# An edge kernel's attribute encoding: two matmuls over 111 rows and 512 columns for four over 30 rows and 256

## The chip, the cores and the metric

The kernel runs on one core of one Trainium2 chip. The metric is the device time of one execution in microseconds; lower is better. Engines: PE (TensorE, matmuls; PEld are its weight loads), DVE (VectorE), ACT (ScalarE), POOL (GpSimd, which here issues the indirect gathers), SP (SyncE, which issues most other DMAs).

## The reference

A graph attention layer over 6250 nodes and 200000 edges sorted by destination, then a mixture of experts that the change does not touch. What matters is the encoding of an edge's three attributes and its use:

```python
h = (x @ W.T).reshape(n, H, D)          # H = 8 heads of 32
alpha = einsum(h_src, a_src) + einsum(h_dst, a_dst)
enc = relu(edge_attr @ edge_W.T + edge_b).reshape(-1, H, D)
alpha = alpha + jnp.sum(enc * h_dst, axis=-1)
alpha = where(alpha >= 0, alpha, 0.2 * alpha)
attn = softmax of alpha over the edges of one dst
out = segment_sum(h_src * attn[..., None], dst)
```

## The kernel before

Edges are laid out in rows of W = 4 ways: a row belongs to one node, a block has P = 128 rows, that is SLOTS = 512 edge slots, and there are 440 blocks. A step of the edge loop handles Q = 4 blocks, so there are 110 steps, written out one after another; GROUPS = 4 groups of 128 blocks hold the tables.

**Attributes.** To keep f32 precision in bf16, an attribute is split in three bf16 parts (`part_attrs`: cast, subtract, cast, subtract, cast), which gives KA = 9 rows a slot. `store_attrs` writes them with one DMA to `block_attr` in DRAM, as 9 rows of 512 slots for each block; the slots of a row's four ways lie side by side. `load_attr` of the edge loop brings a step's 9 x 2048 values in three times (36 KB each), under each other into `attrT`; with three rows of ones for the bias that makes KE = 30 rows. `keep["expander"]` holds the weights [30, 256] in three bf16 parts, copied there by six small DMAs of POOL.

**PE.** `front(q, b)` encodes block b of step q: for each way k it takes the 128 slots of that way (every fourth column of `attrT`) as stationary operand and `expander` as moving operand, four matmuls of 256 columns (L1036) into the PSUM tiles p_enc, two to a tile, a semaphore after each pair. Then it picks the block's node rows with a one-hot matmul, p_pick (L1043). `add_up` (L1065) sums the weighted source rows, four f32 matmuls a block. PE's order in a step is fixed: turn_rows, front(1), add_up of the step before (2), turn_back, front(2), add_up (3), front(3), add_up(0), front of the step after, add_up(1).

**DVE.** `front` multiplies p_enc by the node rows `near` (L1210, two a block) and reduces (L1214); `scores`, `scan`, `fall` and four `weigh` (L1260) follow in a fixed order. After each of the first 19 steps of every 32, `expand` works on the next group's table: 16 parts of moving words and attributes, then `part_attrs` (L204, L206, L208). ACT copies p_pick to `near` (L1132), makes the one-hot matrices and copies sums. POOL gathers 16 times a step (L1003) and waits for `near` and `weighted`. SP loads two steps ahead and stores the sums; at step 22 of each group it stores the next group's table (L120 to L128) once DVE has made it.

**Prologue.** It ends on group 0: `part_attrs` in ids_in's memory (L204), SP's L128, then the table of bases out (L375) and back (L377), a wait for all table stores, and the edge loop begins with DVE's memset of attrT to ones (L1388), for which SP's first loads wait. Earlier, POOL issues the copies to `expander` (L445, L446) between two gathers (L434, L439); the second needs `run_i` from DVE (L693).

Of the kernel before, what the change touches and what calls it, by code (L numbers as in the profile page):

```python
# [59 lines left out]
KE = 3 * (KA + 1)  # L60
# [64 lines left out]
def store_attrs(nc, scr, b0, n, parts, stored):  # L125

    block = bass.ds(b0, n) if not isinstance(b0, int) else slice(b0, b0 + n)
    nc.sync.dma_start(scr["block_attr"].rearrange("c (b s) -> b c s", s=SLOTS)[block, :, :], parts[0:n, :, :]).then_inc(stored, 16)  # L128
# [69 lines left out]
def part_attrs(nc, x, i, attrs, parts):  # L198


    of = parts[:, EF * i:EF * (i + 1), :]
    x.wait()
    if i < 2:
        x.link(nc.vector.tensor_copy(of, attrs))  # L204
        x.wait()
        x.link(nc.vector.tensor_tensor(attrs, attrs, of, ALU.subtract))  # L206
    else:
        x.link(nc.vector.tensor_copy(of, attrs))  # L208


def prologue(nc, a, scr, keep):

    with Scope(nc) as m:
# [47 lines left out]
        enc_left = m.sb("enc_left", [KA + 1, D])  # L261
# [30 lines left out]
            dummy_made dummy_stored bias_loaded merge_consts""".split()  # L292
# [29 lines left out]
        def _(sp):  # L322
# [56 lines left out]
            sp.wait_ge(s["table_stored"], 64)  # L379
# [3 lines left out]
        def _(pool):  # L383
# [10 lines left out]
            ins.then_inc(s["consts_made"], 1)  # L394
            nc.gpsimd.memset(ones[:, :], 1.0).then_inc(s["consts_made"], 1)
# [46 lines left out]

            pool.wait_ge(s["enc_split"], 4)
            for j in range(3):
                pool.dma_start(keep["expander"][KA * j:KA * (j + 1), :], enc_p[0:KA, j, :]).then_inc(s["enc_moved"], 16)  # L445
                pool.dma_start(keep["expander"][3 * KA + j:3 * KA + j + 1, :], enc_p[KA:KA + 1, j, :]).then_inc(s["enc_moved"], 16)  # L446
# [13 lines left out]
            pool.wait_ge(s["enc_moved"], 96)  # L460
# [227 lines left out]


# [109 lines left out]
def edge_loop(nc, a, scr, keep):  # L799

    with Scope(nc) as m:
        rec = m.sb("rec_in", [P, RING, Q, W + 1])
        rec_i = rec[:, :, :, :].bitcast(I32)
        attrT = m.sb("attrT", [KE, RING, Q, SLOTS], BF16)
# [77 lines left out]
        def _(sp):  # L882
# [10 lines left out]
            def load_attr(q):  # L893
                if q.since(RING):
                    sp.wait_ge(s["enc"], PAIRS * Q * (q.prev().s))
                cols = scr["block_attr"].rearrange("c (n e) -> n c e", e=Q * SLOTS)
                v = block_of(cols, q.s)
                for j in range(3):
                    sp.dma_start(attrT[KA * j:KA * (j + 1), q.par, :, :].rearrange("c q e -> c (q e)"), v).then_inc(s_attr[q.par], 16)
# [74 lines left out]
            for i in range(GROUPS - 1):  # L974
                for u in range(turn):
                    if u == LOADED_AT:
                        sp.wait_ge(s["table_stored"], 64 * (i + 1))
                    body(straight(RING + i * turn + u))
                    if u == STORED_AT:
                        store_group(i, P)  # L980
# [42 lines left out]
        def _(pe):  # L1023
            def front(q, b):
# [5 lines left out]
                for half in range(PAIRS):  # L1030
                    if PAIRS * b + half >= len(p_enc) or q.since(1):
                        pe.wait_ge(s["prod"], PAIRS * n + half + 1 - len(p_enc))
                    for j in range(2):
                        k = 2 * half + j
                        slots = attrT[:, q.par, b, :].rearrange("c (r k) -> c k r", k=W)[:, k, :]
                        last = nc.tensor.matmul(p_enc[(PAIRS * b + half) % len(p_enc)][:, j, :], slots, keep["expander"][:, :], start=True, stop=True)  # L1036
                    last.then_inc(s["enc"], 1)
# [163 lines left out]
        def _(dve):  # L1201
# [129 lines left out]
            def expand(i, k):  # L1331
# [12 lines left out]
                elif k == 2 * WAY_BITS:  # L1344
                    if i:
                        dve.wait_ge(s["table_stored"], 64 * i)
# [613 lines left out]
def build(nc, a, out):  # L1960
    def dram(name, shape, dt=F32):
# [4 lines left out]
               block_flags=dram("block_flags", (GROUPS * P, H, P)), block_places=dram("block_places", (GROUPS * P, P)), block_attr=dram("block_attr", (KA, GROUPS * P * SLOTS), BF16),  # L1966
# [11 lines left out]
def edge_part(nc, a, scr, whole):  # L1978
    with Scope(nc) as m:
        keep = dict(  # L1980
            whole, node_at=m.sb("node_at", [P, P]), expander=m.sb("expander", [KE, D], BF16),
# [45 lines left out]
```

## Time and profile before

| | |
|---|---|
| median of 3 runs | 3568.86 us (3564.5 to 3572.67) |
| the profiled execution | 3549.46 us |
| its span, first to last instruction | 3547.7 us |
| PE busy (matmuls) | 2421.1 us, 68% |
| PEld busy | 1634.9 us, 46% |
| DVE busy | 2273.3 us, 64% |
| ACT busy | 986.2 us, 28% |
| POOL busy | 1904.2 us, 54% |
| mean granted clock of PE | 0.763 of 2.4 GHz |
| edge loop | about 181 to 2990 us |

Busy time is from one profiled execution. Matmuls are pipelined and their ends are modelled, so the busy time of PE counts overlapping latency. What ended an idle stretch is inferred; "issue" is a wait that nothing in the profile explains.

### The profile page before, as it was taken

To read this page: it belongs to the slowest core of one execution; us is meant where nothing else is said; L and a number is where in the kernel's file an instruction comes from. 1 tells how busy PE (TensorE), PEld (TensorE's weight loads), DVE (VectorE), ACT (ScalarE), POOL (GpSimd) and SP (SyncE) were. 2 spreads that over 40 slices of the span, in tenths; PEclk is the share of its full clock that TensorE was granted. 3 is DMA by queue.
4 is the path that set the end of the run, shared out by engine and by line. 5 is a ranking of instruction groups with operands and counts; after the bars stand their busy time and mean duration, and the time that the engine had idled before them with its cause. 6 is when DMAs were issued, how large, how long until landed. Compare 5 with 4: busy or idle time off the path is not lost. (4 is left out here: it accounts for less than half of the span.)

```text
span 3547.7 us, 36332 instructions
## 1 busy us (share of the span) xinstructions
PE 2421.1 (68%) x8642; PEld 1634.9 (46%) x8642; DVE 2273.3 (64%) x3546; ACT 986.2 (28%) x2822; POOL 1904.2 (54%) x2041
## 2 busy tenths in 40 slices
PE   1647667776667667676677767777676554269998
PEld 1424444444444444444444444444444333168887
DVE  7957767776667677776667777776666554251223
ACT  3522222222222222222222222222222221043332
POOL 3656656666666566666666656666666442607000
PEclk9857777777778677877777777777777676559999
DMA  8355555556555555556555555556556883300000
GB/s 270 124 136 153 154 147 153 150 149 178 147 154 154 144 155 145 159 149 177 151 152 154 150 150 155 147 156 174 150 154 134 124 121 53 88 27 3 21 18 31
DMA packets 341609, 471.12 MB, mean 133 GB/s; under 512 B 115596, under 2 KB 262718, under 8 KB 341170
## 3 DMA queue, kind: packets, MB, share of 16 engines
q0 software_dynamic: 90000, 262.14, 30.0%
q1 hardware_dynamic: 250578, 206.73, 20.0%
q8 instruction: 60, 0.98, 0.1%
q14 instruction: 123, 1.01, 0.1%
q10 hardware_dynamic: 848, 0.26, 0.0%
HBM read 380.17 MB, written 88.72 MB: 132 GB/s over the span
## 5 line engine op out<-in xcount | busy, mean ns | idle before, releaser
L1003 POOL DMA_INDIRECT src_in<-t_node_rows,rec_in x1760 | 1681.5, 955 | 1112.4 <-issue 552.2
L1065 PE MATMUL p_sum<-weighted,hot 128*128 128x264 f32 x3520 | 1262.5, 520 | 610.5 <-issue 420.9
L1065 PEld LDWEIGHTS p_sum<-weighted,hot 128*128 128x128 f32 x3520 | 875.2, 259 | 975.6 <-issue 703.7
L1210 DVE SCALAR_TENSOR_TENSOR prod<-p_enc,near 128x512 f32<-128x512 f32 x880 | 563.1, 680 | 421.7 <-ACT near L1132 355.8
L1260 DVE TENSOR_TENSOR weighted<-src_in,p_turn 128x1024 f32<-128x1024 f32 x440 | 534.5, 1215 | 326.6 <-remote 129.8
L1214 DVE TENSOR_REDUCE dots<-prod 128x32 f32<-128x1024 f32 x440 | 536.9, 1220 | 15.2
L1043 PE MATMUL p_pick<-win,hotT 128*128 128x272 f32 x880 | 383.2, 523 | 192.5 <-ACT near L1132 88.3
L1112 ACT ACTIVATE hot<-apart 128x128 f32<-128x128 f32 x440 | 136.2, 309 | 1336.5 <-issue 543.8
L1132 ACT COPY near<-p_pick 128x272 f32<-128x272 f32 x440 | 169.4, 385 | 680.4 <-remote 391.3
L1036 PE MATMUL p_enc<-expander,attrT 30*128 30x256 bf16 x1760 | 314.7, 305 | 43.2 <-DMA attrT<-t_block_attr 42.9
L1043 PEld LDWEIGHTS p_pick<-win,hotT 128*128 128x128 f32 x880 | 154.2, 220 | 301.7 <-issue 200.9
L1036 PEld LDWEIGHTS p_enc<-expander,attrT 30*128 30x128 bf16 x1760 | 174.5, 121 | 190.8 <-issue 121.0
L1699 PE MATMUL p_up<-x2T,w 128*128 (+2 forms) x800 | 175.5, 378 | 9.3 <-DMA b<-in_L_ffn_b 9.3
L1108 ACT ACTIVATE apart<-node_at,rec_in 128x128 f32<-128x128 f32 x440 | 175.7, 399 | 0.0
L1709 PE MATMUL p_y<-w,act_h 128*128 128x256 f32 x784 | 173.1, 379 | 0.0
L1153 ACT COPY sums<-p_sum 128x264 f32<-128x264 f32 x440 | 158.2, 359 | 27.7 <-PE p_sum L1065 27.6
L1699 PEld LDWEIGHTS p_up<-x2T,w 128*128 128x128 f32 x800 | 151.1, 192 | 29.9 <-DMA b<-in_L_ffn_b 9.4
L1896 DVE TENSOR_TENSOR acc<-acc,p_y 128x256 f32 (+1 forms) x49 | 20.6, 421 | 218.7 <-PE p_y L1709 218.7
L1709 PEld LDWEIGHTS p_y<-w,act_h 128*128 128x128 f32 x784 | 148.9, 190 | 20.2
L1776 ACT ACTIVATE act_h<-p_up,b 128x256 f32<-128x256 f32 (+1 forms) x200 | 91.7, 468 | 158.9 <-PE p_up L1699 157.9
L1119 ACT ACTIVATE places<-places,after_p 128x512 f32<-128x512 f32 x110 | 79.7, 725 | 45.9 <-DMA places<-t_block_places 43.1
L1671 PE MATMUL p_T<-ident,acc 128*128 128x128 f32 x98 | 33.2, 442 | 80.3 <-issue 64.8
(334 smaller groups left out, 1623.5 us busy)
## 6 DMA issues: line engine op xcount, KB each, us to landing
win<-t_node_rows SPq DMA_DIRECT2D x440, 136.0 KB
t_block_sums<-sums SPq DMA_DIRECT2D x110, 528.0 KB
places<-t_block_places SPq DMA_DIRECT2D x110, 256.0 KB
src_in<-t_node_rows,rec_in POOLq DMA_INDIRECT x1760
attrT<-t_block_attr SPq DMA_DIRECT2D x330, 36.0 KB
t_node_rows<-out_rows SPq DMA_DIRECT2D x49, 136.0 KB, 1.7
x<-in_x SPq DMA_DIRECT2D x4, 1536.0 KB, 25.6
out_x<-x SPq DMA_DIRECT2D x48, 128.0 KB
```

The lines of the kernel that those rows point to most:

```text
L1003: pool.indirect_dma_start(src[:, q.par, b, k, :], None, scr["rows"], bass.IndirectOffsetOnAxis(ap=rec_i[:, q.par, b, k:k + 1], axis=0)).th ...
L1036: last = nc.tensor.matmul(p_enc[(PAIRS * b + half) % len(p_enc)][:, j, :], slots, keep["expander"][:, :], start=True, stop=True)
L1043: nc.tensor.matmul(p_near, hotT[:, q.par, b, :], win[:, q.par, b, :], start=True, stop=True).then_inc(s["picked"], 1)
L1065: last = nc.tensor.matmul(p_sum[b % 2][:, 0:ROW], hot[:, q.par, b, :], weighted[:, b, k, :], start=(k == 0), stop=(k == W - 1))
L1108: nc.scalar.activation(apart[:, :], keep["node_at"][:, :], ACT.Abs, bias=rec[:, q.par, b, W:W + 1]).then_inc(s["apart"], 1)
L1132: nc.scalar.copy(near[:, q.par, b, :], p_near).then_inc(s["near"], 1)
L1153: nc.scalar.copy(sums[:, q.par, b, :], p_sum[b % 2][:, 0:ROW]).then_inc(s["sums"], 1)
L1210: nc.vector.scalar_tensor_tensor(prod[:, 2 * half:2 * half + 2, :], p_enc[(PAIRS * b + half) % len(p_enc)][:, :, :], 0.0, near[:, q.par, b ...
L1214: nc.vector.tensor_reduce(dots[:, q.par, b, :, :].rearrange("p k h -> p (k h)"), prod[:, :, :].rearrange("p k (h d) -> p (k h) d", h=H), A ...
L1260: nc.vector.tensor_tensor(heads(weighted[:, b, :, 0:D]), heads(src[:, q.par, b, :, 0:D]), spread(p_weight[:, b, :, :], HD), ALU.mult).then ...
L1699: last = nc.tensor.matmul(p_up[n % 4][:, 0:cols], w1[:, k, i, f * P:(f + 1) * P], x, start=(i == 0), stop=(i == 1))
L1709: last = nc.tensor.matmul(p_y[u][:, :], act_h[:, b, n, u * P:(u + 1) * P], w2[:, k, f, :], start=(n == 0), stop=(n == TOPK * hidden - 1))
```

## The change

The four ways of a slot row become rows of the contraction. `block_attr` gets W x KA = 36 rows of 128 columns a block in place of 9 rows of 512, `attrT` 3 x 37 = 111 rows in place of 30, and `expander` becomes block diagonal, [111, 1024], zero elsewhere: way k's weights stand in columns 256 k to 256 k + 255. One matmul of 512 columns encodes two ways, and two matmuls a block replace four. DVE writes the bf16 parts sorted by way, reading its attributes with a step of four elements. The store becomes four DMAs, one a way. POOL clears `expander` and fills it with 24 DMAs in place of six. Memory of `enc_left` is laid into `ro`, with a wait on DVE ahead of ro's use.

```diff
-KE = 3 * (KA + 1)
+KE = 3 * (W * KA + 1)
+STORES = 3 + W
@@ store_attrs
-    nc.sync.dma_start(scr["block_attr"].rearrange("c (b s) -> b c s", s=SLOTS)[block, :, :], parts[0:n, :, :]).then_inc(stored, 16)
+    table = scr["block_attr"].rearrange("(k c) (b r) -> k b c r", k=W, r=P)
+    for k in range(W):
+        nc.sync.dma_start(table[k, block, :, :], parts[0:n, :, k * P:(k + 1) * P]).then_inc(stored, 16)
@@ part_attrs
-    of = parts[:, EF * i:EF * (i + 1), :]
+    of = parts[:, EF * i:EF * (i + 1), :].rearrange("p f (k r) -> p f k r", k=W)
+    attrs = attrs.rearrange("p f (r k) -> p f k r", k=W)
@@ prologue
-        enc_left = m.sb("enc_left", [KA + 1, D])
+        enc_left = ro[0:KA + 1, :, :].rearrange("p r w -> p (r w)")[:, 0:D]
@@ SP
-            sp.wait_ge(s["table_stored"], 64)
+            sp.wait_ge(s["table_stored"], 16 * STORES)
@@ POOL
+            nc.gpsimd.memset(keep["expander"][:, :], 0.0).then_inc(s["enc_zero"], 1)
             pool.wait_ge(s["enc_split"], 4)
+            pool.wait_ge(s["enc_zero"], 1)
             for j in range(3):
-                pool.dma_start(keep["expander"][KA * j:KA * (j + 1), :], enc_p[0:KA, j, :]).then_inc(s["enc_moved"], 16)
-                pool.dma_start(keep["expander"][3 * KA + j:3 * KA + j + 1, :], enc_p[KA:KA + 1, j, :]).then_inc(s["enc_moved"], 16)
+                for k in range(W):
+                    row = KA * (W * j + k)
+                    pool.dma_start(keep["expander"][row:row + KA, k * D:(k + 1) * D], enc_p[0:KA, j, :]).then_inc(s["enc_moved"], 16)
+                    row = KA * W * 3 + j
+                    pool.dma_start(keep["expander"][row:row + 1, k * D:(k + 1) * D], enc_p[KA:KA + 1, j, :]).then_inc(s["enc_moved"], 16)
-            pool.wait_ge(s["enc_moved"], 96)
+            pool.wait_ge(s["enc_moved"], 96 * W)
@@ DVE, after the statistics of x
+            dve.wait_ge(s["enc_split"], 4)
@@ edge_loop
-        attrT = m.sb("attrT", [KE, RING, Q, SLOTS], BF16)
+        attrT = m.sb("attrT", [KE, RING, Q, P], BF16)
@@ load_attr
-                    sp.dma_start(attrT[KA * j:KA * (j + 1), q.par, :, :].rearrange("c q e -> c (q e)"), v).then_inc(s_attr[q.par], 16)
+                    sp.dma_start(attrT[W * KA * j:W * KA * (j + 1), q.par, :, :].rearrange("c q e -> c (q e)"), v).then_inc(s_attr[q.par], 16)
@@ front of PE
-                    for j in range(2):
-                        k = 2 * half + j
-                        slots = attrT[:, q.par, b, :].rearrange("c (r k) -> c k r", k=W)[:, k, :]
-                        last = nc.tensor.matmul(p_enc[(PAIRS * b + half) % len(p_enc)][:, j, :], slots, keep["expander"][:, :], start=True, stop=True)
-                    last.then_inc(s["enc"], 1)
+                    nc.tensor.matmul(p_enc[(PAIRS * b + half) % len(p_enc)][:, :, :].rearrange("p j d -> p (j d)"), attrT[:, q.par, b, :],
+                                     keep["expander"][:, 2 * half * D:(2 * half + 2) * D], start=True, stop=True).then_inc(s["enc"], 1)
@@ build, edge_part
-block_attr=dram("block_attr", (KA, GROUPS * P * SLOTS), BF16),
+block_attr=dram("block_attr", (W * KA, GROUPS * P * P), BF16),
-expander=m.sb("expander", [KE, D], BF16),
+expander=m.sb("expander", [KE, W * D], BF16),
```

## Rows read from the trace of the kernel before

**Rows 1.** Groups by line and form, 1000 to 2000 us: busy, mean ns | idle before
```profile
L1003 POOL DMA_INDIRECT src_in<-t_node_rows,rec_in x648 | 619.7, 956 | 380.8 <-issue 214.7 <-ACT near L1132 124.6 <-DVE weighted L1260 41.5
...
L1036 PE MATMUL p_enc<-expander,attrT 30*128 30x256 bf16 x648 | 114.6, 303 | 0.0
...
L1036 PEld LDWEIGHTS p_enc<-expander,attrT 30*128 30x128 bf16 x648 | 64.2, 121 | 54.1 <-issue 44.6 <-DVE prod L1210 1.7
```

**Rows 2.** Busy by stretch: us, PE, PEld, DVE, ACT, POOL, clock, DMA share, GB/s
```profile
261.30:737.90 476.60, 336.26 (x1106) 212.53 (x1106) 350.74 (x503) 129.50 (x403) 294.04 (x306) 0.74 0.55 151
737.90:1052.90 315.00, 221.33 (x755) 141.70 (x754) 216.74 (x299) 86.72 (x271) 195.02 (x206) 0.76 0.56 158
...
1842.70:2313.10 470.40, 335.45 (x1110) 211.13 (x1110) 350.87 (x504) 128.75 (x401) 292.34 (x304) 0.75 0.55 152
2313.10:2632.50 319.40, 229.91 (x746) 146.52 (x746) 217.20 (x299) 87.14 (x273) 197.10 (x208) 0.73 0.56 158
```

**Rows 3.** Timeline from 1602 us: start us, us, engine, line [idle before <-releaser]
```profile
1602.24 0.39 ACT L1132 COPY near<-p_pick 128x272 f32<-128x272 f32 x1 [5.03 <-remote]
...
1605.12 1.21 DVE L1260 TENSOR_TENSOR weighted<-src_in,p_turn 128x1024 f32<-128x1024 f32 x1
...
1606.43 0.78 PE L1065 MATMUL p_sum<-weighted,hot 128*128 128x264 f32 x1 [3.03 <-issue]
```

**Rows 4.** Timeline of p_enc and p_pick at both clocks; then p_enc's min/median/max
```profile
1504.53 0.62 PE L1036 MATMUL p_enc<-expander,attrT 30*128 30x256 bf16 x4
...
1505.08 0.73 PE L1043 MATMUL p_pick<-win,hotT 128*128 128x272 f32 x2
...
1526.00 1.04 PE L1036 MATMUL p_enc<-expander,attrT 30*128 30x256 bf16 x4
...
1526.97 1.27 PE L1043 MATMUL p_pick<-win,hotT 128*128 128x272 f32 x2
...
L1036 PE MATMUL p_enc<-expander,attrT x648: 265/268/416, 1000.3 to 1996.1; 30*128 30x256 bf16 x162
```

**Rows 5.** Groups by line and form over the whole span, p_turn on PE
```profile
L1049 PE MATMUL p_turn<-ident,row_top 128*32 128x128 f32 x110 | 35.1, 319 | 68.5 <-issue 43.1 <-DVE row_top L1230 25.2
...
L1054 PE MATMUL p_turn<-ident,tops 32*128 32x32 f32 x110 | 30.6, 278 | 0.7 <-issue 0.7
```

**Rows 6.** Timeline at the end of the prologue, DVE and SP's queue
```profile
153.74 0.95 DVE L204 CAST ids_in<-work 128x1536 bf16<-128x1536 f32 x1
...
154.73 1.76 DVE L206 TENSOR_TENSOR work<-work,ids_in 128x1536 f32<-128x1536 f32 x1
...
160.43 0.37 SPq L128 DMA_DIRECT2D t_block_attr<-ids_in  x1
...
174.20 0.24 SPq L377 DMA_DIRECT2D base_i<-t_block_bases  x1
...
177.06 3.47 DVE L1388 MEMSET attrT<- 30x4096 bf16 x1 [5.43 <-PEq L213]
```

**Rows 7.** Timeline, DVE: a contiguous pass and one reading each sixth element
```profile
163.38 0.69 DVE L716 TENSOR_TENSOR kept_planes<-kept_planes,work 128x512 int32<-128x512 int32 x1
...
164.17 1.05 DVE L708 SCALAR_TENSOR_TENSOR work<-rec,slot_at 128x512 f32<-128x512 f32 x1
```

**Rows 8.** Timeline of POOL: last of the six copies, first gather of runs
```profile
63.91 0.50 POOL L446 DMA_DIRECT2D expander<-enc_p  x1
74.61 1.06 POOL L439 DMA_INDIRECT rec<-t_edge_records,run_i  x1 [10.21 <-DVE run_i L693]
```

**Rows 9.** DMA issues, 155 to 180 us: count, KB each, us to landing
```profile
t_block_attr<-ids_in SPq DMA_DIRECT2D x1, 1152.0 KB, 8.3
t_block_flags<-flags SPq DMA_DIRECT2D x1, 512.0 KB, 3.4
...
t_block_bases<-base_int SPq DMA_DIRECT2D x1, 2.0 KB, 13.3
```

**Rows 10.** Waits of SP's own queue, whole span: us in total, times, longest
```profile
SPq L925 <- ACT sums L1153: 374.4, 43, 34.5
```

More of the change, by code:

```diff
@@ L291, in prologue @@
             attrs_out based moved attr_made rows_out table_stored base_made base_stored base_loaded
-            dummy_made dummy_stored bias_loaded merge_consts""".split()
+            dummy_made dummy_stored bias_loaded merge_consts enc_zero""".split()
         s = {n: m.sem("s_" + n) for n in names}
@@ L895, in load_attr @@
                     sp.wait_ge(s["enc"], PAIRS * Q * (q.prev().s))
-                cols = scr["block_attr"].rearrange("c (n e) -> n c e", e=Q * SLOTS)
+                cols = scr["block_attr"].rearrange("c (n e) -> n c e", e=Q * P)
                 v = block_of(cols, q.s)
                 for j in range(3):
-                    sp.dma_start(attrT[KA * j:KA * (j + 1), q.par, :, :].rearrange("c q e -> c (q e)"), v).then_inc(s_attr[q.par], 16)
+                    sp.dma_start(attrT[W * KA * j:W * KA * (j + 1), q.par, :, :].rearrange("c q e -> c (q e)"), v).then_inc(s_attr[q.par], 16)
             def load_flags(q):
@@ L976, in _ @@
                     if u == LOADED_AT:
-                        sp.wait_ge(s["table_stored"], 64 * (i + 1))
+                        sp.wait_ge(s["table_stored"], 16 * STORES * (i + 1))
                     body(straight(RING + i * turn + u))
@@ L1345, in expand @@
                     if i:
-                        dve.wait_ge(s["table_stored"], 64 * i)
+                        dve.wait_ge(s["table_stored"], 16 * STORES * i)
                     make_rows_of(nc, x, words, group(keep["base"]), group(keep["base_mod"]), small, ro, head_flags, item[:, i + 1, 1:2], group(last_ok))
@@ L1965, in build @@
                records=dram("edge_records", (P * EPP + UNIT, REC)), block_rows=dram("block_rows", (GROUPS * P, P * (W + 1))),
-               block_flags=dram("block_flags", (GROUPS * P, H, P)), block_places=dram("block_places", (GROUPS * P, P)), block_attr=dram("block_attr", (KA, GROUPS * P * SLOTS), BF16),
+               block_flags=dram("block_flags", (GROUPS * P, H, P)), block_places=dram("block_places", (GROUPS * P, P)), block_attr=dram("block_attr", (W * KA, GROUPS * P * P), BF16),
                bases=dram("block_bases", (GROUPS * P,), I32),
@@ L1980, in edge_part @@
         keep = dict(
-            whole, node_at=m.sb("node_at", [P, P]), expander=m.sb("expander", [KE, D], BF16),
+            whole, node_at=m.sb("node_at", [P, P]), expander=m.sb("expander", [KE, W * D], BF16),
             base_i=m.sb("base_i", [1, BLOCKS], I32), tops=m.sb("block_tops", [Q * H, STEPS, 2]),
```

## Prediction

> **What bounds the kernel now.** First the busy rows of 1000 us in the middle of the edge loop, by line and form [rows 1]. No engine is full. POOL's gathers take 956 ns each and sit 0.30 us apart (648 x 0.30 = 194 of the 214.7 us put down to issue), so the 16 gathers of a step of four blocks need 16 x 1.256 = 20.1 us. The stretches cut at the starts of steps [rows 2] show how long a step really is: 13 steps without other work take 313.2 to 319.4 us, 24.3 us on the mean of the three. So POOL is near, but something else sets four of the 24 us. The timeline shows a ring through three engines [rows 3]: ACT's `near` (1602.24) releases DVE, which does prod, reduce and, in its fixed order, `weighted` of another block (1605.12 to 1606.33); that releases PE's p_sum (1606.43); and behind p_sum, in PE's fixed order, stand the next p_enc, p_pick and with it the next `near`. p_enc lies in this ring wherever PE comes late, with the time from its start to that of p_pick, not with its summed busy time of 114.6 us [rows 1], since its matmuls overlap.
>
> How much does added work on one engine of this ring cost? The loop holds a measurement: 19 steps of each group carry the unpacking of the next group on DVE, 13 don't [rows 2]. There are six such stretches, of which four stand there; the middle two last 476.6 and 313.2 us with DVE busy 350.7 and 216.5. DVE is busy 1052.3 / 57 = 18.46 us in the ones and 650.5 / 39 = 16.68 in the others; the steps last 1423.6 / 57 = 24.98 and 947.6 / 39 = 24.30 us. 1.78 us of DVE work cost 0.68 us: a coupling of 0.38.
>
> **1. Four matmuls of 256 columns become two of 512 (loop, gain).** The columns stay 1024 a block. At the full clock four take 0.62 us to the end of the last, whose own median is 0.268 in the trace's rows and mean 303 ns here [rows 1, 4]: with 0.268, three spacings are 0.352, one 0.117 us, where 256 columns at 2.4 GHz are 0.107. So some 0.010 us a matmul is not columns, and two fewer save 0.02 us a block: p_pick would follow after 0.53 instead of 0.55 us (1504.53 to 1505.08). At the low clock (1526.00) p_pick follows after 0.97 us, of which 4 x 0.213 = 0.85 are columns; the rest is ahead of p_pick and stays: nothing saved. The granted clock of 0.73 to 0.78 [rows 2] means the full level for about half of the time. Gain: 440 x 0.5 x 0.02 = 4.4 us, taken at full price because p_enc is in the ring: **-4**. Bounds: 0, and the weight loads laid bare. 880 loads at 99 ns (64.2 us / 648 [rows 1]) are 87 us, times 0.38 is 33. I stay near the low end since the spacing of 0.117 leaves no room for a bare load of 0.1. That 111 rows are contracted instead of 30 costs nothing: p_turn's two transposes differ by 96 rows and by 96 columns and only by 41 ns, 319 against 278 [rows 5], and 96 columns at 2.4 GHz are 40 ns.
>
> The Trainium skill (TensorE: Matmul & The Clock Gate, Back-to-back issue gap) has the warm gap as the columns at 2.4 GHz plus about 2.5 ns. By that rule, which speaks against the change, two matmuls fewer save 5 ns a block, an estimate of about 1 us in all; the spacing of 0.117 us in [rows 4] is wider than the rule's.
>
> **2. The bf16 parts are cut by way (DVE, loss).** Per group three casts of 1536 elements at 0.95 us and two subtractions at 1.76 us [rows 6] now read the attributes with a step of four floats, and the subtraction writes so too. The cast runs at nearly twice the rate of the subtraction now, and may fall to it. The nearest rows of stepped reads: 512 elements six floats apart take 1.05 us against 0.69 for the contiguous pass of the same size [rows 7], so 0.7 ns an element more. Bounds for a group: 0, and casts that lose both (to 2.9 us) with subtractions 1.1 us longer, 3 x 1.9 + 2 x 1.1 = +7.9. I take casts a little slower than today's subtractions and those nearly unchanged: 3 x 1.0 + 2 x 0.2 = +3.4 us, since a step of four floats is closer to dense than one of six. In the prologue this is bare, because SP's store waits for it: **+3.4**. The three groups in the loop pay 3 x 3.4 x 0.38 = **+3.9**.
>
> **3. One store of 1152 runs of 1 KB becomes four stores of 4608 runs of 256 B in all (loss).** Issue: three more at 0.37 us [rows 6], **+1.1** in the prologue, where the base table's store is queued behind it and the launch of the edge part waits for that (L377 at 174.20). Moving data: the attribute store lands 8.3 us after issue for 1152 KB, the flags in runs of 512 B 3.4 us for 512 KB [rows 9]: 7.2 and 6.6 ns per KB, so runs of 512 B cost nothing visible. For 256 B there is no row. Bounds: 0, and the price per run of the 4-byte store below (rival 3). I take **+2**, by the nearest row, the flags, with a little for four times the runs. In the loop SP has slack: it stood 374.4 us before the sums' stores in the trace [rows 10]; the extra issue is hidden there, and if that cover were gone it would cost 3 x 1.1. Queued behind the stores are the next steps' rec, places, attrT and window loads; I take **+2** for three groups together (0 to 3 x 3). The wait counts change with the stores and add no wait of their own. attrT's loads stay three of 36 KB.
>
> **4. Prologue, the rest.** The memset of attrT goes from 4096 to 1024 elements a partition, 3.47 us to about 0.9 [rows 6]; SP's first load of the loop waits for exactly this: **-2.6** (-3 to 0). POOL issues 24 small copies to the expander instead of 6, 18 x 0.50 = 9 us more; they ended at 64.4, so now at 73.4, and POOL waited 10.21 us there for run_i before 74.61 [rows 8]. **0**, with 1.2 us of cover left; if the new memset of expander or slower copies eat it, +1 to +2. The new wait of DVE for enc_split holds nothing: what it waits for is DVE's own work, done before the statistics. The memset of expander on POOL (about 0.5 us near 4 us) delays loads that are used some 40 us later: 0. enc_left in ro is memory only.
>
> **Sum.** Prologue 3.4 + 1.1 + 2 - 2.6 + 0 = +3.9; loop -4.4 + 3.9 + 2 = +1.5; together about +5 us on the profiled run of 3549.5 us (span 3547.7), 3555. That run lies 19 us below the median of 3568.9; I carry the difference over: **3573 us**, +0.1%. What a measurement of this kernel can tell from no change is about 0.2%, 7 us.
>
> **Rivals.**
> 1. *The weight loads are bare in the ring* (faster). If a pair of load and matmul costs PE its load wherever p_enc begins after a wait, and that is most blocks, the loop gains up to 33 us: 3573 + 4 - 33 = 3544; at half, 3560. For it: p_enc is in the ring, and PE idles 54.1 us before its loads. Against: the spacing of 0.117 us [rows 4].
> 2. *DVE's stepped passes cost what six floats apart cost* (slower). +7.9 a group. It decides as soon as a cast takes over about 2.3 us: prologue +4.5 more than in the sum, and in the loop, if the passes stand bare between two steps instead of at 0.38, 3 x 7.9 = 24 instead of 3.9: 3573 + 4.5 + 20 = 3598. For it: unpacking stands between the last `weighted` of a step and the scores of the next. Against: the coupling of 0.38.
> 3. *Short runs to memory are slow* (slower). The table of bases, 512 runs of 4 bytes, issued right behind the attributes, landed 13.3 us after its issue, that is at 174.2 where L377 starts, 5.5 us after the attributes landed (160.43 + 8.3) [rows 6, 9]. At that 10.7 ns a run, 4608 runs take 49 us, 41 more than now; the prologue pays them all, and each of three stores in the loop holds up the loads behind it by about 30: 3573 + 41 + 90 = about 3700. At 2 ns a run (9.8 us) it is nothing. Against: 512-byte runs keep the rate. The Trainium skill (DMA: Bandwidth & Descriptors, Specifications) says that transfers below 512 B are not at line rate, because the DMA engine then reads, modifies and writes. It speaks for this rival, and no row here has a 256 B run to memory.
> 4. *The change shortens nothing on PE*: columns bound it at both clocks, only costs stay: 3577. It is inside the forecast's own range.
>
> **Chances.** Forecast with rival 4: 0.53, own range 3558 to 3584 (gain 0 to 15, DVE 0 to +10, stores 0 to +6). Rival 1: 0.22. Rival 2: 0.17. Rival 3: 0.08. Faster by over 0.2% (below 3562): rival 1 and 0.06 of the forecast, 0.28. Slower (above 3576): rivals 2 and 3 and 0.09 of the forecast, 0.34. Within: 0.38. The range, 3546 to 3600, leaves out rival 3, the far half of rival 1 and a little of rival 2, some 0.2 together.
>
> **What the new profile would show.** p_enc: 880 matmuls of 30 -> 111 rows and 512 columns, p_pick 0.53 us after the first (0.97 at the low clock); if 0.45 or less, rival 1. Casts at L204 near 2 us, subtractions near 1.95; casts at 2.9 mean rival 2. In the prologue the store's landing about 10 us and base_i's load 6 us later than 174.2; 40 later is rival 3. POOL's first run gather within 1 us of 74.6. Steps of 24.3 us without unpacking, unchanged to 0.1. I am wrong in kind if those plain steps move by over 0.3 us, since 0.3 x 110 is 33 us.

## The result: slower by 0.7%, and the profile after

| | before | after |
|---|---|---|
| median, side by side (6 runs each) | 3569.19 us | 3599.96 us |
| ratio | | 1.0073, 95% interval 1.0047 to 1.0100 |
| the profiled execution | 3549.46 us | 3583.28 us |
| PE busy | 2421.1 us | 2207.7 us |
| DVE busy | 2273.3 us | 2301.2 us |
| mean granted clock of PE | 0.763 | 0.80 |
| first scores (`raw`), last scores | 213.38, 2967.6 us | 221.45, 3002.01 us |

The forecast was 3573 us and "within 0.2%". The time came out at 3600, slower, next to rival 2's 3598. The scores of a step are one DVE instruction, `raw`, so its starts cut the loop: from the first of its 110 starts to the last it is 2780.6 us, 26.4 more than before, and the prologue grew by 8.1. The rest of the span is the same (579.5 us against 580.1).

The profile after, page rows (busy, mean ns | idle before, releaser):

```profile
PE 2207.7 (62%) x7762; PEld 1529.1 (43%) x7762; DVE 2301.2 (64%) x3546; ACT 980.4 (27%) x2822; POOL 1917.5 (54%) x2060
...
L1221 DVE SCALAR_TENSOR_TENSOR prod<-p_enc,near 128x512 f32<-128x512 f32 x880 | 562.5, 680 | 287.8 <-ACT near L1143 221.2
```

PE has 213 us less to do and DVE 28 us more, and the sign of the result follows DVE. The end of the prologue, timeline of DVE, POOL and SP's queue after (start us, us; answers to [rows 6] and [rows 8]):

```profile
76.38 1.00 POOL L447 DMA_INDIRECT rec<-t_edge_records,run_i  x1 [0.30 <-issue]
...
155.71 2.84 DVE L210 CAST ids_in<-work 128x1536 bf16<-128x1536 f32 x1
...
158.59 2.87 DVE L212 TENSOR_TENSOR work<-work,ids_in 128x1536 f32<-128x1536 f32 x1
...
170.27 3.30 SPq L132 DMA_DIRECT2D t_block_attr<-ids_in  x4
...
185.65 0.24 SPq L384 DMA_DIRECT2D base_i<-t_block_bases  x1
187.59 0.91 DVE L1399 MEMSET attrT<- 111x1024 bf16 x1 [6.12 <-PEq L219]
...
188.79 0.38 SPq L905 DMA_DIRECT2D rec_in<-t_block_rows  x1
```

The same first load in the timeline before:

```profile
180.83 0.37 SPq L891 DMA_DIRECT2D rec_in<-t_block_rows  x1
```

The chain reads off by differences. The parts begin 1.97 us later (155.71 against 153.74). The store's issue comes 9.84 later (170.27 against 160.43), so the passes took 7.87 us more. The load of the base table comes 11.45 later, so the store's part took 1.6 more. The memset's start is 10.53 later, its length 2.56 less, and SP's first load 7.96 later. A cast costs 2.84 for 0.95 and a subtraction 2.87 for 1.76: 3 x 1.89 + 2 x 1.11 = 7.9 us a group, the figure of rival 2.

In the loop the parts lie in the 18th and 19th step of each group of 32. Stretches cut at the starts of those two steps in the third group (busy us and count of PE, PEld, DVE, ACT, POOL, then clock, DMA share, GB/s), before:

```profile
2266.57:2290.22 23.65, 20.51 (x61) 12.01 (x60) 19.16 (x25) 6.77 (x21) 15.74 (x17) 0.66 0.53 143
2290.22:2313.12 22.90, 14.86 (x58) 9.58 (x58) 20.33 (x29) 6.09 (x20) 16.15 (x15) 0.85 0.59 158
```

and after:

```profile
2308.09:2334.41 26.32, 17.18 (x50) 11.01 (x50) 22.17 (x26) 6.10 (x19) 18.10 (x18) 0.74 0.55 158
2334.41:2361.26 26.85, 14.31 (x50) 9.29 (x50) 25.09 (x29) 7.26 (x23) 18.34 (x19) 0.80 0.58 156
```

DVE was busy 20.3 us in the second of them already, more than in any other of the 32 steps (16.5 to 19.3) and more than POOL's 16 gathers need (20.1); with 4.8 us on top it is busy 25.1 of 26.9. How much of that the step pays these two executions can't say: before, the same step took 27.4, 26.7 and 22.9 us in the three groups, after 27.0, 27.5 and 26.9, among steps that scatter between 18 and 30 us in both. The experiments on chips without this scatter show it.

PE's timeline after, at both clocks (answers to [rows 4]):

```profile
1605.22 0.60 PE L1047 MATMUL p_enc<-expander,attrT 111*128 111x512 bf16 x2
1605.65 0.62 PE L1054 MATMUL p_pick<-win,hotT 128*128 128x272 f32 x2
...
1639.48 1.03 PE L1047 MATMUL p_enc<-expander,attrT 111*128 111x512 bf16 x2
1640.31 0.84 PE L1054 MATMUL p_pick<-win,hotT 128*128 128x272 f32 x2
```

p_pick now starts 0.43 us after p_enc at the full clock instead of 0.55, and 0.83 to 0.85 instead of 0.97 at the low one. That is 0.12 us a block, six times the saving I had worked out and on rival 1's side of the mark of 0.45. At 440 blocks it is 53 us of PE, and the time shows no gain.

### The profile page after: what moved, and what is told of

It reads as the page before. It is cut to its first block and busy times, and to the rows that moved or that the text cites. A ratio compares the mean times of both kernels' runs of the same rounds, so it can differ in the third digit from the quotient of the medians.

```text
span 3581.5 us, 34606 instructions
## 1 busy us (share of the span) xinstructions
PE 2207.7 (62%) x7762; PEld 1529.1 (43%) x7762; DVE 2301.2 (64%) x3546; ACT 980.4 (27%) x2822; POOL 1917.5 (54%) x2060
## 3 DMA queue, kind: packets, MB, share of 16 engines
q1 hardware_dynamic: 274494, 206.73, 20.3%
## 5 line engine op out<-in xcount | busy, mean ns | idle before, releaser
L1076 PE MATMUL p_sum<-weighted,hot 128*128 128x264 f32 x3520 | 1171.6, 490 | 851.9 <-issue 477.6
L1076 PEld LDWEIGHTS p_sum<-weighted,hot 128*128 128x128 f32 x3520 | 810.6, 241 | 1190.5 <-issue 802.2
L1054 PE MATMUL p_pick<-win,hotT 128*128 128x272 f32 x880 | 319.1, 447 | 135.7 <-ACT near L1143 67.1
L1047 PE MATMUL p_enc<-expander,attrT 111*128 111x512 bf16 x880 | 312.2, 441 | 49.7 <-DMA attrT<-t_block_attr 42.3
L1054 PEld LDWEIGHTS p_pick<-win,hotT 128*128 128x128 f32 x880 | 191.6, 223 | 242.2 <-issue 111.0
L1164 ACT COPY sums<-p_sum 128x264 f32<-128x264 f32 x440 | 158.7, 361 | 26.7 <-PE p_sum L1076 26.6
L1720 PEld LDWEIGHTS p_y<-w,act_h 128*128 128x128 f32 x784 | 148.9, 190 | 20.2
L1047 PEld LDWEIGHTS p_enc<-expander,attrT 111*128 111x128 bf16 x880 | 86.6, 109 | 116.5 <-DMA attrT<-t_block_attr 42.7
L1060 PE MATMUL p_turn<-ident,row_top 128*32 128x128 f32 x110 | 32.4, 294 | 119.5 <-issue 69.1
```

The costliest lines, as they stand in the source:

```text
L1047: nc.tensor.matmul(p_enc[(PAIRS * b + half) % len(p_enc)][:, :, :].rearrange("p j d -> p (j d)"), attrT[:, q.par, b, :], keep["expander"][ ...
L1054: nc.tensor.matmul(p_near, hotT[:, q.par, b, :], win[:, q.par, b, :], start=True, stop=True).then_inc(s["picked"], 1)
L1076: last = nc.tensor.matmul(p_sum[b % 2][:, 0:ROW], hot[:, q.par, b, :], weighted[:, b, k, :], start=(k == 0), stop=(k == W - 1))
L1164: nc.scalar.copy(sums[:, q.par, b, :], p_sum[b % 2][:, 0:ROW]).then_inc(s["sums"], 1)
L1720: last = nc.tensor.matmul(p_y[u][:, :], act_h[:, b, n, u * P:(u + 1) * P], w2[:, k, f, :], start=(n == 0), stop=(n == TOPK * hidden - 1))
```

## The experiments

Three theories stood at first. **A**: the loss is the stepped passes and the prologue, and PE's gain counts for little. **B**: the two matmuls lengthen the plain steps. **C**: the loads of 36 x 1 KB do. The kernels ran on four chips. The kernel before takes 3569, 3532, 3063 and 3065 us on them, so each kernel is compared with the kernel before on its own chip, and a ratio is given with its 95% interval.

**Four matmuls, 111 rows** (`four_matmuls`): two 256-column matmuls in place of each 512-column one, all else as changed.

```diff
-  nc.tensor.matmul(p_enc[...][:, :, :], attrT[:, q.par, b, :], keep["expander"][:, 2 * half * D:(2 * half + 2) * D], ...)
+  for j in range(2):
+      k = 2 * half + j
+      last = nc.tensor.matmul(p_enc[...][:, j, :], attrT[:, q.par, b, :], keep["expander"][:, k * D:(k + 1) * D], ...)
```

> The changed kernel with four matmuls of 256 columns a block over its 111 rows, in place of two of 512; all else as changed, same result. It undoes the one part that should gain. Theory A (the two matmuls shorten PE by about 0.12 us a block, p_pick now follows p_enc's start after 0.43 in place of 0.55 us, and the ring passes some of it on; the loss comes from DVE's stepped passes and the prologue): slower than the changed kernel by 5 to 25 us, about 3610 against 3600, and p_pick follows after 0.55 us. Theory B (the two matmuls themselves lengthen the plain steps of the loop, from 24.3 to 24.7 us, by a chain that the profile does not name): faster than the changed kernel by up to 25 us, plain steps back at 24.3. Theory C (the loads of 36 runs of 1 KB lengthen them): as the changed kernel within 7 us.

Measured: 3546.70 us, 1.0033 (1.0012 to 1.0055), clock 0.80. That looked a little better than the 1.0073 of the changed kernel, on another chip, whose interval it touches. It had to be run beside it (below).

**Dense passes** (`dense_parts`): part_attrs as in the kernel before, so the attributes reach the matmuls in another order than computed for; every count and size is that of the changed kernel.

```diff
-    of = parts[:, EF * i:EF * (i + 1), :].rearrange("p f (k r) -> p f k r", k=W)
-    attrs = attrs.rearrange("p f (r k) -> p f k r", k=W)
+    of = parts[:, EF * i:EF * (i + 1), :]
```

> The changed kernel with the three casts and two subtractions of a group read and written in dense order as before; the bf16 parts then stand in the wrong order in memory, so the encoded attributes belong to other edges; all instructions, stores and loads are otherwise as in the changed kernel. Theory A: the prologue gives back 7.9 us, and the three groups in the loop 3 x 7.9 times the coupling of 0.38 that unpacking had before, 9 us, together 17 us below the changed kernel, about 3583. If DVE's passes stand bare in the loop: 32 us below, about 3568. Theory B and C: only the prologue's 8 and the small coupled part come back, and plain steps stay at 24.7 us.

Measured: 3530.11 us, 1.0007 (0.9985 to 1.0028). The loss is gone with the step of four floats. Against the four matmuls on the same chip, which had stepped passes, it is 16.6 us by the medians and 9 by the ratios (0.0026 x 3532).

**The kernel before with the new loads** (`before_narrow_loads`): the table as 36 rows, three loads of 36 x 1 KB and four stores with runs of 1 KB, while the matmuls still contract 30 rows (the values in them are not the right slots').

```diff
-  sp.dma_start(attrT[KA * j:KA * (j + 1), q.par, :, :], v)            # 9 rows of 4 KB
+  sp.dma_start(attrT_all[W * KA * j:W * KA * (j + 1), q.par, 0:Q * P], v)   # 36 rows of 1 KB
```

> The kernel before with attrT's loads in the shape of the changed kernel, three of 36 runs of 1 KB in place of three of 9 runs of 4 KB; PE still reads 30 partitions and 4 KB of each, of which most holds ones, so the encoded attributes are wrong. The table's store is four DMAs of 32 partitions with runs of 1 KB. Theory C (the loads' shape lengthens every step): slower than before by 20 to 50 us, plain steps at 24.7. Theories A and B: within 7 us of before (3569), plus 1 us for three more issues in the prologue.

Measured: 3531.57 us, 1.0011 (0.9986 to 1.0036). C falls.

**POOL's 24 copies behind the gathers of runs** (`late_expander`).

```diff
@@ POOL, ahead of the gathers of runs
-            (the waits for enc_split and enc_zero and the 24 copies to expander)
             for g in range(GROUPS):
                 gather_runs(g)
+            (the same waits and copies)
```

> The changed kernel with POOL's 24 copies to the expander issued behind the gathers of runs in place of ahead of them, same result. All theories: the gathers start at 74.4 in place of 76.4 us, so the prologue is 2 us shorter if nothing behind the copies is late in turn: POOL's copies of the attributes out of the gathered runs start up to 12.6 us later than they could, and DVE's moves of attributes wait for the first of them. If that is late, the prologue is up to 8 us longer. 3598 or 3606.

Measured: 3564.94 us, 1.0082 (1.0050 to 1.0113): nothing gained. POOL now makes the attribute copies, for which DVE waits, only after the 24 issues. Its timeline:

```profile
75.27 1.01 POOL L447 DMA_INDIRECT rec<-t_edge_records,run_i  x1 [12.47 <-DVE run_i L707]
...
97.46 2.96 POOL L467 COPY work<-rec 128x1536 f32<-128x1536 f32 x1
```

The first `raw` stands at 230.2 us, 8.7 later than in the changed kernel. With no copies ahead of it the first gather still starts at 75.27, because DVE's `run_i` is not there earlier. So in the changed kernel (76.38) the copies cost at most about 1 us.

**All four versions side by side.** The changed kernel, the two versions with one part undone, and the one with both undone, on one chip where the kernel before takes 3063.53 us.

> The changed kernel as it is, beside three relatives on the same chip and in the same rounds. Its ratio to before was 1.0073 (1.0047 to 1.0100) on another chip. All theories: 1.005 to 1.009 again.

> The changed kernel with four matmuls of 256 columns over 111 rows, same result; its ratio to before was 1.0033 (1.0012 to 1.0055) in the first call, where the changed kernel itself was not run. Theory B (two matmuls of 512 columns cost time in the loop): 0.3 to 0.5% below after_again. Theory A (they gain a little or nothing, and the first difference was one between chips): at or above after_again, within 0.2% at least.

> The changed kernel with dense casts and subtractions (bf16 parts in the wrong order in memory, so the encoded attributes belong to other edges). First ratio to before 1.0007. If the passes cost 8 us in the prologue and are bare in the loop, 32 us or 0.9% below after_again; if coupled at 0.38, 17 us or 0.5%.

> Both undone: dense passes and four matmuls (parts in the wrong order as in dense_again). Theory B: 0.3 to 0.5% below dense_again and so faster than before by 0.3%. Theory A: within 0.2% of dense_again or above it.

| | us | ratio (95%) | loop | plain step | last two part steps |
|---|---|---|---|---|---|
| two matmuls, stepped | 3090.59 | 1.0094 (1.0080 to 1.0108) | 2321.1 | 20.08 | 23.9, 27.1 |
| four matmuls, stepped | 3092.92 | 1.0097 (1.0082 to 1.0111) | 2323.3 | 20.08 | 23.9, 27.1 |
| two matmuls, dense | 3058.09 | 0.9982 (0.9973 to 0.9991) | 2296.1 | 20.02 | 20.8, 22.1 |
| four matmuls, dense | 3056.23 | 0.9984 (0.9974 to 0.9993) | 2289.2 | 19.99 | 20.9, 22.2 |

Loop and steps are differences of `raw`'s starts in the profiled executions, the part steps means of three groups. Two or four matmuls make no difference, with stepped or with dense passes: B falls, and so does any gain from that part of the change, and the 1.0033 of four matmuls above belongs to a chip whose steps scatter. (The one kernel with two matmuls and stepped passes that ran there, `late_expander`, has 1.0082, of which its later start is 0.0025; the 0.0024 left between the two are less than their intervals together, 0.004.) The stepped passes cost 3090.59 - 3058.09 = 32.5 us with two matmuls, and 3092.92 - 3056.23 = 36.7 with four. Their place is seen in two timelines of DVE, the 18th step of the first group. Two matmuls, stepped:

```profile
625.43 1.21 DVE L1271 TENSOR_TENSOR weighted<-src_in,p_turn 128x1024 f32<-128x1024 f32 x1
626.56 2.89 DVE L210 CAST l_parts<-kept_planes 128x1536 bf16<-128x1536 f32 x1
629.48 2.86 DVE L212 TENSOR_TENSOR kept_planes<-kept_planes,l_parts 128x1536 f32<-128x1536 f32 x1
632.26 0.28 DVE L1233 TENSOR_TENSOR raw<-dots,src_in 128x128 f32<-128x128 f32 x1
```

Two matmuls, dense:

```profile
617.43 1.21 DVE L1270 TENSOR_TENSOR weighted<-src_in,p_turn 128x1024 f32<-128x1024 f32 x1
618.56 1.04 DVE L209 CAST l_parts<-kept_planes 128x1536 bf16<-128x1536 f32 x1
619.64 1.76 DVE L211 TENSOR_TENSOR kept_planes<-kept_planes,l_parts 128x1536 f32<-128x1536 f32 x1
621.32 0.28 DVE L1232 TENSOR_TENSOR raw<-dots,src_in 128x128 f32<-128x128 f32 x1
```

No line names an idle time: last `weighted`, passes and scores stand end to end, and each us of the passes moves the scores. From `weighted` to `raw` it is 6.83 us in the one and 3.89 in the other. The two part steps grow by 3.1 and 5.0, 8.1 us a group: the whole 7.9 is paid. In the next step next to nothing is given back (18.8 us, and with dense passes 19.2 with two matmuls, 18.4 with four). DVE's busy time alone does not say so: with dense passes it is busy 19.1 us in the first of the two steps, 1.0 less than POOL's 20.1, and of the 3.0 us that come on top 3.1 are paid all the same, because the passes stand in the chain from `weighted` to the scores.

**The stepped passes alone in the kernel before** (`before_stepped_parts`), another chip, kernel before 3064.51 us: the two rearrangements of the diff under "Dense passes", added to the kernel before.

> The kernel before with the five stepped passes alone: its parts are cut by way, all else (one store, 30 rows, four matmuls) is as it was, so the attributes reach the matmuls in another order, and the output changes. Theory A: +7.9 us in the prologue and 3 x 7.9 in the loop, +32 us: 1.009 to 1.010 of the kernel before, nearly the whole loss of the changed kernel. Rival (coupling of 0.38): +8 and +9 = +17 us, 1.005. The part steps of each group grow by 3 and 5 us, the plain steps stay.

Measured: 3093.83 us, 1.0090 (1.0075 to 1.0106), +29.3 us; plain steps 20.06, the last two part steps 23.2 and 26.7. The five passes alone carry nearly the whole loss, and the rival of +17 us by a coupling of 0.38 falls.

**A fifth matmul in each block of the kernel before** (`before_five`).

```diff
                         last = nc.tensor.matmul(p_enc[...][:, j, :], slots, keep["expander"][:, :], start=True, stop=True)
+                        if k == 3:
+                            last = nc.tensor.matmul(p_enc[...][:, j, :], slots, keep["expander"][:, :], start=True, stop=True)
```

> The kernel before with a fifth matmul of 256 columns in each block, which writes once more what the fourth wrote; the output is the same. PE has some 0.11 us more a block at the full clock (0.21 at the low one) between p_enc's start and p_pick, 440 x 0.11 = 48 us or more. Theory A (PE's time in p_enc passes to the step only by a small part, since POOL's gathers bound it): at most +10 us, 1.003 or less. Rival (p_enc bare in the ring, as the prediction took it): +48 us or more, 1.014 or more. Coupled at 0.38: +18 us, 1.005.

Measured: 3069.22 us, 1.0010 (0.9997 to 1.0023), +5 us. From p_enc to p_pick it is now 0.66 us instead of 0.55:

```profile
1503.35 0.62 PE L1036 MATMUL p_enc<-expander,attrT 30*128 30x256 bf16 x4
1503.82 0.27 PE L1038 MATMUL p_enc<-expander,attrT 30*128 30x256 bf16 x1
1504.02 0.72 PE L1045 MATMUL p_pick<-win,hotT 128*128 128x272 f32 x2
```

0.11 x 440 = 48 us of PE, or more where the clock is low, moved the time by 5, at the interval's upper end (0.0023 x 3064) by 7: a coupling of 0.1, at most 0.15. On this chip PE is not in the ring as I had it.

**Runs of 1 KB to memory** (`long_runs`): dense passes, and the four stores split by blocks and not by way, so 1152 runs of 1 KB in place of 4608 of 256 B (the attributes land in yet another order).

```diff
+    table = scr["block_attr"].rearrange("(k c) (b s) -> k b c s", k=W, s=SLOTS)
     for k in range(W):
-        nc.sync.dma_start(table[k, block, :, :], parts[0:n, :, k * P:(k + 1) * P])
+        rows = slice(k * (n // W), (k + 1) * (n // W))
+        nc.sync.dma_start(table[k, b0 // W:b0 // W + n // W, :, :], parts[rows, :, :])
```

> The changed kernel with dense passes, and its four stores writing 1152 runs of 1 KB in all in place of 4608 of 256 B; the number of stores, their bytes and the loads are the same. The attributes come out in another order. Theory: short runs cost the 0.5 to 1 us that is left of the +1.6 us of the store's part in the prologue after three more issues at 0.37, so against the kernel with dense passes alone (0.998 to 1.001 of before) this is the same to 0.1%. Rival (short runs slow the memory or the loads behind them in the loop): 10 us or more faster than the dense passes alone, 0.997 or less on a slow chip.

Measured: 3051.06 us, 0.9945 (0.9931 to 0.9959), where the dense passes with short runs had 0.9982 (0.9973 to 0.9991) on the other chip of that speed. My theory of "the same to 0.1%" falls: the intervals don't meet. DMA issues in the prologue, short runs and then long ones (count, KB each, us to landing):

```profile
t_block_attr<-ids_in SPq DMA_DIRECT2D x4, 288.0 KB, 4.1
t_block_bases<-base_int SPq DMA_DIRECT2D x1, 2.0 KB, 12.0
```

```profile
t_block_attr<-ids_in SPq DMA_DIRECT2D x4, 288.0 KB, 4.6
t_block_bases<-base_int SPq DMA_DIRECT2D x1, 2.0 KB, 8.9
```

The base table behind the stores lands 3.1 us sooner, and from the stores' issue to the base load it is 12.4 us instead of 15.35. But what the loop's loads wait for is the memset of attrT, and from the stores' issue to its start it is 16.04 us instead of 17.28 (17.28 with four matmuls too): only 1.2 us of the 0.37% (11 us) come out of the prologue this way. In the loop the long runs took 2291.4 us, the short ones 2296.1 and, with four matmuls, 2289.2, and the steps with the stores show no pattern. Where the other 10 us are, or whether the change of chip makes them, stays open; the two did not run beside each other.

**One stepped pass in place of five** (`step_once`), the same output as the changed kernel. A stepped copy lays the attributes by way as f32 into the memory of the later parts, the casts and subtractions are dense, and the bias rows of a way go to the expander in one copy, 16 issues in all.

```diff
+    of = parts[:, EF * i:EF * (i + 1), :]
+    if i == 0:
+        by_way = parts[:, EF:, :].rearrange("p f s -> p (f s)").bitcast(F32).rearrange("p (f s) -> p f s", f=EF)
+        x.link(nc.vector.tensor_copy(by_way.rearrange("p f (k r) -> p f k r", k=W), attrs.rearrange("p f (r k) -> p f k r", k=W)))
+        x.wait()
+        x.link(nc.vector.tensor_copy(of, by_way))
+        x.wait()
+        x.link(nc.vector.tensor_tensor(attrs, by_way, of, ALU.subtract))
@@ POOL
-                    pool.dma_start(keep["expander"][row:row + 1, k * D:(k + 1) * D], enc_p[KA:KA + 1, j, :])
+            for k in range(W):
+                pool.dma_start(keep["expander"][KA * W * 3:, k * D:(k + 1) * D], enc_p[KA:KA + 1, :, :])
```

> The changed kernel with one stepped pass a group in place of five: a copy of the attributes to f32 in way order (into the memory of the later parts), then three casts and two subtractions over dense memory; and the three bias rows of a way go to the expander in one copy, so that POOL issues 16 copies and not 24. The output is the same. Theory A (the stepped passes stand bare between two steps and cost what their records show): the passes of a group take 2.84 + 3 x 0.95 + 2 x 1.76 = 9.2 us in place of 14.3, so 5.1 us less a group, all four groups bare: -20 us against the changed kernel, with the copies up to 4 us less in the prologue, so -20 to -24 us. With the changed kernel at 1.0073 to 1.0095 of the kernel before, that is 1.001 to 1.003. Rival (the coupling of 0.38 that the prediction took from whole steps): prologue -5, loop 3 x 5.1 x 0.38 = -6: 1.005 or more.

Measured: 3068.70 us, 1.0009 (1.0000 to 1.0018). Theory A's 1.001 to 1.003 just about holds (it came out at its good end), the rival's 1.005 does not. Its passes in the prologue:

```profile
156.59 2.85 DVE L210 COPY ids_in<-work 128x1536 f32<-128x1536 f32 x1
159.47 0.96 DVE L212 CAST ids_in<-ids_in 128x1536 bf16<-128x1536 f32 x1
160.47 1.76 DVE L214 TENSOR_TENSOR work<-ids_in 128x1536 f32<-128x1536 f32 x1
```

The last two part steps are 24.0 and 22.1 us: the first still holds the stepped copy, the second has lost its 5 us. The loss of 0.9% is down to 0.1%. The two edits, the one copy and the fewer issues, were not run apart. It doesn't beat the kernel before. Long runs in the table as well (by block, and 256 B runs in the loads instead) might; that was not run.

## Why the prediction was wrong

**Step 2, the stepped passes, is the term that failed, twice over.** The price: I took a cast from 0.95 to about 1.95 us and left a subtraction nearly unchanged, because four floats seemed closer to dense than six. They took 2.84 and 2.87. (2.84 - 0.95) / 1536 is 1.2 ns an element more for the cast and (2.87 - 1.76) / 1536 is 0.7 for the subtraction: the same 0.7 ns of the row with six floats [rows 7]. The shorter distance saved nothing, and the cast fell to the subtraction's rate. So +7.9 a group, not +3.4, as the upper bound had it.

The coupling: I gave the loop's three groups 0.38 of that, +3.9 us in all. On the chips with 3063 and 3065 us it was all of it, 24: prologue and loop together are 32.5 and 36.7 us by the dense kernels, 29.3 by the stepped passes alone in the kernel before. The 0.38 was an average over 19 steps, most of whose unpacking has room on DVE. Cut at single steps, the same trace of before has DVE busy 20.3 us in the one that gets 4.8 us more, over POOL's 20.1, and the other is paid as the passes stand in the chain to the scores. So the term is 7.9 + 24 = 32 us, where the sum had 7.3, and the 25 us between are as large as all but 2 of the 27 from 3573 to 3600.

On the chip with 3532 us, whose steps scatter, the stepped passes cost 16.6 us by the medians and 9 by the ratios, with an interval of about 11 either way (0.0022 of each, taken together). That alone fits a coupling of 0.38, 17 us in all, better than one. But `late_expander`, stepped too, stands 34.8 us above the dense kernel on the same chip by the medians and 26.5 by the ratios, 26 and 18 without the 8.7 of its later start. So on this chip the price lies between the two couplings and is not settled. On the chip of the result, which scatters too, the changed kernel stood alone, and its 30.8 us (0.0073, with 0.0026 either way) fit the full price but don't prove it. So the full coupling is shown where POOL paces the steps; where stalls leave room it may be less, and that stays open.

The Trainium skill (VectorE: DVE Perf Modes, What auto-detection actually checks) ties the double rate of an op with one source to operands in SBUF whose outermost sizes are even or equal, not to the step of an f32 operand. By that rule the cast would have kept its 0.95 us; it took 2.84, and the measurement decides.

**Step 1, PE, had the size too small and its worth too large.** The mark for rival 1 was reached (0.43 us), but not by fewer matmuls. With four matmuls over 111 rows, p_pick follows just as soon:

```profile
1510.61 0.60 PE L1049 MATMUL p_enc<-expander,attrT 111*128 111x256 bf16 x4
1510.94 0.30 PEld L1057 LDWEIGHTS p_pick<-win,hotT 128*128 128x128 f32 x2
1511.05 0.62 PE L1057 MATMUL p_pick<-win,hotT 128*128 128x272 f32 x2
```

And in the kernel before, over 30 rows:

```profile
1594.19 0.62 PE L1036 MATMUL p_enc<-expander,attrT 30*128 30x256 bf16 x4
1594.74 0.30 PEld L1043 LDWEIGHTS p_pick<-win,hotT 128*128 128x128 f32 x2 [0.19 <-issue]
1594.74 0.72 PE L1043 MATMUL p_pick<-win,hotT 128*128 128x272 f32 x2
```

Over 111 rows p_pick's weight load starts 2 ns after the fourth p_enc matmul (1510.94) and is hidden behind it. Over 30 rows it starts 0.20 us after it, only with p_pick itself. So the load that lay bare in this stretch was p_pick's, where rival 1 counted p_enc's own, and the number of matmuls has no part in it. The 0.117 us that I took for the spacing of the four came from a modelled end: their starts are 0.137, 0.109 and 0.109 us apart, so there was no 0.010 us in each matmul to be saved. From the fourth to p_pick it is 0.198 us over 30 rows and 0.109 over 111, and between p_pick's own two matmuls 0.333 and 0.232.

The other neighbours of p_enc show the same. These are medians of how long after the start of a matmul the weight load of the next one starts, back to back, in the traces of before and `after_again`. Where both contract few rows (30 or 32) or both many (111 or 128) it is 0.002 us: p_enc to p_enc in both kernels, p_sum (128 rows) to p_enc over 111, p_turn of `tops` (32 rows) to p_enc over 30. Where they differ it is 0.314 us from p_sum to p_enc over 30 rows, so p_enc's first load lay bare too, and 0.239 from that p_turn to p_enc over 111. p_enc of the kernel before also reads its slots with a step of four, but p_turn's 32 rows are read without a step and behave alike, so the rows are the cause that fits both. Here step 1 erred in putting the 111 rows at nothing: it held the lengths of two matmuls against each other and not what stands between one of few rows and one of many.

It pays nothing, since PE does not set the step: on the chips without the scatter p_enc 48 us longer costs 5 us, and two matmuls in place of four gain nothing. On the chip with 3532 us the kernel with dense passes over 111 rows (1.0007) and the one with the new loads over 30 (1.0011) are the same too. The -4.4 of the sum was in truth about 0.

**What sets the plain step.** I read four of its 24.3 us as a ring of ACT, DVE and PE above POOL's 20.1. On the chips with 3063 and 3065 us the same code has plain steps of 20.0 to 20.1, POOL's 16 x 1.256, in the versions of the table, and 19.9 to 20.2 in all eight. So the four us were stalls that come with the chip, not a ring that the code sets. ACT's wait for p_pick from 1000 to 2000 us, first the kernel before (24.3 us a step), then the changed kernel on the chip with 3063:

```profile
L1132 ACT COPY near<-p_pick 128x272 f32<-128x272 f32 x163 | 62.8, 385 | 213.3 <-remote 135.3 <-PE p_pick L1043 45.5 <-issue 32.5
```

```profile
L1143 ACT COPY near<-p_pick 128x272 f32<-128x272 f32 x193 | 74.5, 386 | 178.2 <-PE p_pick L1054 178.2
```

135 us in 1000 are put down to "remote" in the one, and none in the other. The word says that no instruction is recorded as ending where the wait ended; it does not say that the wait was for another core. The semaphore is that of p_pick. The `near` of 1602.24 [rows 3] copies a p_pick whose matmuls are recorded as ended at 1595.46, and ACT had been free since 1597.21. In the whole profile of before 116 of the 440 copies start over 1 us after both, 367 us in all (changed kernel 105, 303 us); in the eight profiles of the chips with 3063 and 3065 us none does. So these stalls lie between the recorded end of PE's work and the signal of it. The trace of before also holds only 325 updates of that semaphore, where those chips' traces hold 441. Whether PE ended later than recorded or its signal came late, and why on some chips only, is not shown. The word stood in [rows 3], and I read over it. Of my marks on plain steps (0.1, and 0.3 for wrong in kind) both were passed in the profiled pair, 24.74 against 24.30, but the standard error of each mean is 0.4, so the mark could not be read there. On the chip with 3063 us the versions with two and four matmuls lie within 0.1.

**Step 3, the store**, was +1.6 us in the prologue, where +3.1 stood (1.1 issue, 2 data). Rival 3 fell: behind 4608 short runs the base table lands 3 us later than behind 1152 long ones, not 41. (At 2 ns a run 4608 are 9.2 us, where I wrote 9.8.) With long runs the four stores are 1.4 us quicker to the base load than the one store of before (12.4 against 13.8), which makes up a part. In the loop it is nothing that shows in a step. The 0.994 of the kernel with long runs leaves room for up to 10 us there.

**Step 4, the rest of the prologue.** The memset took 0.91 us, -2.56 as worked out. POOL's copies hold: the first gather came 1.8 us later than before, over my mark of 1 us, but DVE's cast of `run_i` began at 75.62 itself, 1.5 us later than before, so the copies have 0.3 us of it. They were worked out at 0 with a cover of 1.2 us.

**The sum as it was.** In the profiled pair: prologue 2.0 (parts begin later) + 7.9 + 1.6 - 0.9 (between base load and memset) - 2.6 = +8.0. Loop +26.4 in the profiled executions, for which the passes have up to 24; the rest is below what one execution can tell. The difference of the medians was 30.8.

## What to carry to other kernels

An average of how far added work is passed on hides the steps that decide: cut the trace at the very step that gets the work and hold the engine's busy time there against what bounds the step, for at 20.3 us beside POOL's 20.1 there is no cover for another 4.8. Then look where in the engine's order the work stands, for at 19.1 us another 3.0 were paid in full as well. A changed access pattern is priced at the nearest stepped row in full, for every pass that touches it, and it pays to rearrange once, then stay dense. Before a wait is read as a ring between engines, look what the trace names as its releaser, since time put down to "remote" went away with the chip and not with the code. And a spacing is read from the starts of single matmuls, not from ends that are modelled.

## What the runs showed of the hardware

- With a step of four f32 elements DVE takes 2.84 us for a cast of 1536 elements (0.95 dense), 2.85 for a copy f32 to f32 and 2.87 for a subtraction (1.76 dense), which also writes its result with that step.
- Next to p_enc a weight load is hidden behind the matmul ahead of it where both contract few rows (30 or 32) or both many (111 or 128), and lies bare where they differ: from p_enc's fourth matmul to p_pick, 0.198 us at the full clock with 30 rows and 0.109 with 111 and four matmuls, in every run of either kind. p_pick's own two matmuls, unchanged, are 0.333 us apart behind 30 rows and 0.232 behind 111. Nothing between 32 and 111 rows was run.
- The mean granted clock on the chip with 3532 us is 0.768 for 30 rows (kernel before, 26 runs; 0.767 with the new loads) and 0.799 to 0.803 for 111, with two matmuls or four. On the chips without stalls the two ranges meet (0.829 to 0.837 for 30 rows, 0.835 to 0.843 for 111). What joins the two is not shown; the step of four in p_enc's slots went with the rows.
- The same kernel takes 3532 to 3569 us on two chips and 3063 to 3065 on two others. A gather takes 955 to 958 ns on the ones and 957 to 964 on the others; what differs is the stalls between PE's recorded ends and its signals, and the granted clock (the kernel before: 0.763 and 0.768 against 0.832 and 0.830).
